# Four key places, a plan in fewer steps, and another order of layer 0's stores and layer 3's keys

## The reference

```python
x = x + tanh(g_xattn[0]) * L0_xattn(layernorm(x), ctx, ctx, mask)   # no projections, a mask
x = x + tanh(g_ffn[0]) * L0_ffn(layernorm(x), ...)
x = x + tanh(g_xattn[1]) * L1_xattn(layernorm(x), ctx, Wq, bq, Wk, bk, Wv, bv, Wo, bo)
x = x + tanh(g_ffn[1]) * L1_ffn(layernorm(x), Wr, W1, b1, W2, b2)   # top 2 of 8 experts
x = x + tanh(g_xattn[2]) * L2_xattn(layernorm(x), ctx, ...)
x = x + tanh(g_ffn[2]) * L2_ffn(layernorm(x), ...)                  # top 2 of 8 experts
x = x + tanh(g_xattn[3]) * L3_xattn(layernorm(x), ctx, ...)
x = x + tanh(g_ffn[3]) * L3_ffn(layernorm(x), ...)

# attention, every layer:
attn = softmax(einsum('bhqd,bhkd->bhqk', q, k) * scale)
out = einsum('bhqk,bhkd->bqhd', attn, v).reshape(B, S, 256) @ Wo + bo
# experts, layers 1 and 2:
w, ind = top_k(logits, 2)
out = sum over e of combine[:, e] * (gelu(x @ W1[e] + b1[e]) @ W2[e] + b2[e])
```

## Time and profile before

| | us |
|---|---|
| median of 3 runs | 1548.8 |
| fastest and slowest of them | 1547.69, 1549.62 |
| the profiled execution | 1545.74 |
| its span | 1543.9 |

### The profile page before, as it was taken

How to read it: one execution, slowest core, us unless ns; L and a number is a source line. 1 busy time by engine, 2 the same in 40 slices (tenths; PEclk the granted TensorE clock), 3 DMA queues, 4 the chain that set the end, 5 groups by cost and what they waited for, 6 DMA issues and landing times.

```text
span 1543.9 us, 29425 instructions
## 1 busy us (share of the span) xinstructions
PE 1312.7 (85%) x9497; PEld 955.5 (62%) x9524; DVE 960.3 (62%) x2651; ACT 860.8 (56%) x1718; POOL 721.0 (47%) x859
## 2 busy tenths in 40 slices
PE   2789889998998499999999899839999388995985
PEld 1445479855665289999986556628877245664333
DVE  6779753336985643333337688575544278967787
ACT  2456864434886245455535588535555156875564
POOL 4467440005642577777640564258994426532000
PEclk9999999997999699999999799969999798997998
DMA  9978030049761333343247975125444499710001
GB/s 274 285 153 166 12 100 1 1 130 220 137 140 52 103 123 124 117 149 126 76 148 241 222 129 109 35 89 155 147 132 166 146 259 201 141 28 1 0 14 41
DMA packets 116208, 188.86 MB, mean 122 GB/s; under 512 B 21552, under 2 KB 91824, under 8 KB 110256
## 3 DMA queue, kind: packets, MB, share of 16 engines
q0 software_dynamic: 37696, 105.19, 28.9%
q1 hardware_dynamic: 78368, 81.79, 16.8%
HBM read 128.17 MB, written 50.20 MB: 116 GB/s over the span
## 4 chain that ended last, share of the span: by engine, by line
PE 62%; DVE 14%; DMA 7%; POOL 6%; ACT 5%; issue 5%; SPq 1%; ACTq 0%; DVEq 0%; POOLq 0%
PE PS L1094 8%; PE PS L1253 8%; PE PS L1273 8%; PE PS L1047 8%; PE PS L1051 3%; PE PS L1131 2%; PE PS L1265 2%; DMA qk_parts<-q_parts 2%; PE PS L1074 2%; PE PS L1067 2%; PE PS L1107 2%; POOL weights L818 1%; PE PS L1154 1%; DMA y_tokens<-xng,into 1%; PE PS L911 1%
## 5 line engine op out<-in xcount | busy, mean ns | idle before, releaser
L2152 DVE TENSOR_REDUCE nm<-PS 128x2 f32<-128x512 f32 x384 | 250.3, 676 | 42.2 <-PE PS L1047 40.8
L1047 PE MATMUL PS<-stack 48*128 48x256 f32 x1024 | 212.3, 331 | 38.7 <-issue 10.8
L1047 PEld LDWEIGHTS PS<-stack 48*128 48x128 f32 x1024 | 151.6, 204 | 121.0 <-issue 61.6
L1051 PE MATMUL PS<-stack 49*128 49x256 f32 x1024 | 203.9, 322 | 1.0 <-ACT probs L1576 0.6
L1273 PE MATMUL PS<-weights,hh 128*128 x936 | 189.5, 292 | 3.8 <-DVE hl L2481 3.7
L1253 PE MATMUL PS<-weights,xh 128*128 x468 | 169.9, 418 | 11.3 <-DVE xl L2467 5.4
L1576 ACT ACTIVATE probs<-PS 128x512 f32<-128x512 f32 x256 | 145.0, 595 | 36.4 <-PE PS L1074 15.1
L709 POOL DMA_DIRECT2D stack<-mt x128 | 73.1, 571 | 185.4 <-ACT mt L1585 183.8
L1576 ACT ACTIVATE xng<-PS 128x512 f32<-128x512 f32 x256 | 145.3, 595 | 21.8 <-PE PS L1074 12.5
L1273 PEld LDWEIGHTS PS<-weights,hh 128*128 128x128 f32 x936 | 152.7, 193 | 5.4 <-issue 4.9
L1051 PEld LDWEIGHTS PS<-stack 49*128 49x128 f32 x1024 | 143.5, 195 | 10.5 <-ACT probs L1576 4.3
(11 more groups left out here) (335 smaller groups left out, 3079.9 us busy)
## 6 DMA issues: line engine op xcount, KB each, us to landing
stack<-qk_parts POOLq DMA_DIRECT2D x120, 256.0 KB, 4.1
stack<-qk_parts POOLq DMA_DIRECT2D x136, 128.0 KB, 3.7
qk_parts<-stack SPq DMA_DIRECT2D x32, 512.0 KB, 6.6
qk_parts<-q_parts SPq DMA_DIRECT2D x26, 512.0 KB, 5.3
weights<-W_dram POOLq DMA_DIRECT2D x12, 1024.0 KB, 7.0
wide<-ctxT_dram SPq DMA_DIRECT2D x16, 512.0 KB, 8.0
wslot<-y_tokens SPq DMA_DIRECT2D x16, 512.0 KB, 7.4
weights<-W_dram POOLq DMA_DIRECT2D x12, 512.0 KB, 5.1
```

What stands on the lines that cost most here:

```text
L1047: mm = pe.matmul(PS[:, u % 3, to], nat_q[:, at], nat_k, start=True, stop=True)
L1051: mm = pe.matmul(PS[:, 3 + v % 3, to], key_k[:, at], key_q, start=(l > 0 or half == 0), stop=(l > 0), skip_group_check=(l == 0))
L2152: nc.vector.tensor_reduce(nm[:, j % 2, at:at + 2], PS[:, (2 * t + h) % 3, :].rearrange("p (q n) -> p q n", q=2), AX.X, ALU.max, negate=Tru ...
```

## The change

It has four parts.

1. **Four key places, all layers.** `k_part(g)` lays the parts of groups 0 and 1 in the last slot of `stack` and those of 2 and 3 in the slot before. ACT and DVE no longer wait for the store of group g - 2; SP's `store_k` waits for it itself, for the sake of its semaphore. POOL waits for all key stores before it loads batch 2 (before: batch 3).
2. **Layer 0.** q1 stands in `probs` as in the other layers, and its store waits until batch 0 is loaded (stack_first); q2's and q3's halves wait for the rows of quads 0 to 3 (row_in). SP's order is k0 q0 k1 v0 k2 k3 q1, mask 2, q2, mask 3, v1, q3, v2 v3. PE's first scores ask for qlo_done 2, and DVE does the low part of q3 behind the first two maxima. ACT's first exp waits for q1's stores, which until now was so in layers 1 to 3 only.
3. **Planning.** The two choices go through one instruction where they took two; the chain of eight on `tile_e` becomes one comparison on 39 x 8 elements and one sum; `in_row` is made in two halves of 16, and PE multiplies the first while DVE makes the second; `into` moves behind the tables. POOL's gathers ahead wait: the third for the first to land, the fourth for the second, the fifth for the third and fourth, the seventh for the fifth and sixth.
4. **Layer 3.** All four groups' keys and values stand before the adds on PE, ACT and DVE. Layer 2 keeps the order of before.

```diff
+        def k_part(g, r):
+
+            two = stack[:, SLOTS - 1 - g // 2].rearrange("p q c n -> p (q c n)")
+            return two[:, g % 2 * 2048:(g % 2 + 1) * 2048].rearrange("p (r c n) -> p r c n", r=2, c=KC)[:, r]
...
-            if l and g == 1:
+            if g == 1:
                 return probs[:].rearrange("p a n -> p (a n)").rearrange("p (r c n) -> p r c n", r=2, c=KC)[:, r].bitcast(F32R)
...
                 sp.wait_ge(klo_done, GROUPS * l + g + 1)
+                if l or g >= 2:
+                    sp.wait_ge(*stored(k_out, l, g - 2))
...
-                if l and g >= 2:
+                if g >= 2:
                     sp.wait_ge(*stored(q_out, l, g - 2))
                 for r, part in enumerate((q_hi(l, g), q_lo(l, g))):
-                    if l and g == 1 and r == 0:
+                    if g == 1 and r == 0:
                         sp.wait_ge(stack_first, 144 * (l + 1))
-                    if l and g >= 2:
+                    if g >= 2:
                         j = QUADS * l + 2 * (g - 2) + r
                         sp.wait_ge(row_in[j % 4], 16 * (j // 4 + 1))
...
-                if at == 0 and b == SLOTS - 1:
+                if at == 0 and b == SLOTS - 2:
                     for g in range(GROUPS):
                         pool.wait_ge(*stored(k_out, l, g))
...
                     for i in range(AHEAD):
+                        if 2 <= i < 4:
+                            pool.wait_ge(xq_in[i - 2], 16 * l)
+                        elif i >= 4 and i % 2 == 0:
+                            pool.wait_ge(xq_in[i // 2], 32 * l)
                         gather(i, tile_in(i, i % 2)).then_inc(xq_in[i if i < 2 else 1 + i // 2], 16)
...
-                            pe.wait_ge(qlo_done, GROUPS)
+                            pe.wait_ge(qlo_done, 2)
                         pe.wait_ge(klo_done, GROUPS * (l + 1))
...
-                if l and n == 0:
+                if n == 0:
                     pe.wait_ge(qlo_done, GROUPS * (l + 1))
...
-                pe.wait_ge(hot_done, 2 * l - 1)
                 for j in range(2 * TILES):
+                    if j % TILES == 0:
+                        pe.wait_ge(hot_done, 3 * l - 2 + j // TILES)
...
-                if l and v == 0:
+                if v == 0:
                     act.wait_ge(*stored(q_out, l, 1))
...
-                for m in range(2):
-                    then(tt(eq[:, m], eq[:, m], where, ALU.mult))
-                    then(nc.vector.tensor_reduce(posf[:, m, :], eq[:, m], AX.X, ALU.add))
+                then(tt(eq[:], eq[:], where.unsqueeze(1).broadcast_to([P, 2, TILES, 8]), ALU.mult))
+                then(nc.vector.tensor_reduce(posf[:].rearrange("p m t -> p (m t)"), choices, AX.X, ALU.add))
...
-                for e in range(8):
-                    if e == 0:
-                        then(ts(tile_e[:, 0, :], iotas[:, 0:NT], escan[:, es, 0:1], None, ALU.is_ge))
-                    else:
-                        then(nc.vector.scalar_tensor_tensor(tile_e[:, e % 2, :], iotas[:, 0:NT], escan[:, es, e:e + 1],
-                                                            tile_e[:, 1 - e % 2, :], ALU.is_ge, ALU.add))
+                begun = late[:].rearrange("p i d -> p (i d)")[:, 0:8 * NT].rearrange("p (n e) -> p n e", e=8)
+                then(tt(begun, iotas[:, 0:NT].unsqueeze(2).broadcast_to([P, NT, 8]),
+                        upto.unsqueeze(1).broadcast_to([P, NT, 8]), ALU.is_ge))
+                then(nc.vector.tensor_reduce(tile_e[:, 1, :], begun, AX.X, ALU.add))
...
-                keys_low(l + 1, 0)
+                for g in range(GROUPS if l == 2 else 1):
+                    keys_low(l + 1, g)
```

More of the change, by code:

```diff
@@ L411, in q_place @@
         def q_place(l, g):
-            return stored(q_out, l, g - 4 if l and g == 3 else g - 2)
+            return stored(q_out, l, g - 4 if g == 3 else g - 2)
         def rows_of(n, r, g):
@@ L508, in load_v @@
                                      io["ctx"][g * 512:(g + 1) * 512, :].rearrange("(t p) d -> p t d", p=P)).then_inc(x_in[g], 16)
-                    for g in range(GROUPS):
-                        if g == 2:
-                            load_v(0)
-                            sp.wait_ge(mask_done, 1)
-                            load_mask(2)
-                        store_k(0, g)
-                        store_q(0, g)
+                    store_k(0, 0)
+                    store_q(0, 0)
+                    store_k(0, 1)
+                    load_v(0)
+                    store_k(0, 2)
+                    store_k(0, 3)
+                    store_q(0, 1)
+                    sp.wait_ge(mask_done, 1)
+                    load_mask(2)
+                    store_q(0, 2)
                     sp.wait_ge(mask_done, 2)
                     load_mask(3)
-                    for g in range(1, GROUPS):
+                    load_v(1)
+                    store_q(0, 3)
+                    for g in range(2, GROUPS):
                         load_v(g)
@@ L1507, in features @@
                 act.wait_ge(xT_mm, GROUPS * 2 * l + g + 1)
-                if l == 0 and g >= 2:
+                if l == 0 and g == 2:
                     act.wait_ge(*q_place(l, g))
@@ L1545, in project @@
                     u = 2 * l
-                    keys(l, 0)
-                    values(l, 0)
+                    for g in range(GROUPS if l == 3 else 1):
+                        keys(l, g)
+                        values(l, g)
                     for g in range(GROUPS - 1):
-                        keys(l, g + 1)
+                        if l == 2:
+                            keys(l, g + 1)
                         group_roots(u, g)
-                        values(l, g + 1)
+                        if l == 2:
+                            values(l, g + 1)
                         if g == 1:
@@ L2327, in route, with rows_from @@
                 assert k == ROUTE
-            def rows_of_tiles(l, k, first, part, block):
+            def rows_from(l, k, first, part, block):
                 n = part.shape[1]
@@ L2339, in rows_of_tiles, with rows_to @@
                 nc.vector.scalar_tensor_tensor(idx[:, at], block, float(P), tmp(1), ALU.mult, ALU.add).then_inc(idx_done, 1)
+                return k + 2
+            def rows_to(l, k, first, part, block):
+                n = part.shape[1]
+                at = slice(first, first + n)
+                tmp = lambda r: scan[:, 0].rearrange("p t e -> p (t e)")[:, 32 * (r + 1):32 * (r + 1) + n]
                 nc.vector.scalar_tensor_tensor(tmp(2), block, 0.5, pad_row[:, at], ALU.is_lt, ALU.mult).then_inc(route_v[l], 1)
-                dve.wait_ge(route_v[l], k + 3)
-                tt(tmp(0), part, tmp(2), ALU.add).then_inc(route_v[l], 1)
-                dve.wait_ge(route_v[l], k + 4)
+                dve.wait_ge(route_v[l], k + 1)
+                nc.vector.tensor_tensor(tmp(0), part, tmp(2), ALU.add).then_inc(route_v[l], 1)
+                dve.wait_ge(route_v[l], k + 2)
                 nc.vector.scalar_tensor_tensor(into[:, at], block, float(P), tmp(0), ALU.mult, ALU.add).then_inc(placed, 1)
-                return k + 4
+                return k + 2
             def plan(l):
@@ L2451, in plan_late @@
                 dve.wait_ge(idx_mm, 2 * l)
-                rows_of_tiles(l, k, AHEAD, PS[:, 7, 0:rest], PS[:, 7, rest:2 * rest])
+                k = rows_from(l, k, AHEAD, PS[:, 7, 0:rest], PS[:, 7, rest:2 * rest])
+                rows_to(l, k, AHEAD, PS[:, 7, 0:rest], PS[:, 7, rest:2 * rest])
             def sparse(l):
@@ L2521, in sparse @@
                     group_variances(2 * l + 2, g)
-                    if g + 1 < GROUPS:
+                    if g + 1 == GROUPS:
+                        queries(l + 1, 0)
+                    elif l == 1:
                         keys_low(l + 1, g + 1)
-                    else:
-                        queries(l + 1, 0)
                     group_scales(2 * l + 2, g)
```

61 lines of the change are left out of this document (28 added, 33 removed).

## The result

| | before | after |
|---|---|---|
| median, 18 runs each | 1547.76 us | 1537.35 us |
| profiled execution | 1545.74 | 1539.33 |
| ratio, 95% interval | | 0.9931 (0.9916 to 0.9946) |

The kernel is 10.4 us faster by the medians. Two later jobs, on chips 7 and 9, gave 0.9889 (0.9865 to 0.9913) and 0.9935 (0.9908 to 0.9962) for the same two kernels. The forecast was 1537, with a gain of 12.2.

The account below looks back on a forecast made before the run. PE (62% of the span) bounds it, so edits pay only where PE waits at the end of a DVE, DMA or ACT chain. 4 + 1.2 + 0.3 + 1.4 + 5.3 = 12.2 gives 1537 us, range 1530 to 1544.5.

Parts of the forecast that it names:

- Layer 0, 4 forecast: Layer 0: new store order lets q3 land before mask 3, shortening PE's stall; gain 4 us, bounds -2 to 7.5.
- The first steps: Layer 0: scores near 37, q1 landing 15.4 us later at 56.5, first exp at 57.8, 2.6 us late.
- the old stall: Layer 0: PE stood 4.96 us until 81.72 behind POOL's mask 3 wait; stall and slow clock cost 7.3 us.
- the second rival: Layer 0 gives nothing: first exp 7 to 9 us late, freed stall spent; total 1540.6, chance 0.2.
- Planning of layer 1, 1.2 forecast: Layer 1: tables 2.1 us earlier, PE then waits for its first gather; gain 1.2 us, range 0.5 to 2.1.
- Planning of layer 2, 0.3 forecast: Layer 2: waits between POOL's gathers delay the weights, shrinking the front's 1.2 us to 0.3, range -1 to 1.4.
- the front: Layer 2 planning: same earlier start as layer 1, first gather 0.45 us sooner, worth 1.2 us before gather waits.
- Start of layer 2, 1.4 forecast: Layer 2: four places remove DVE's 1.39 us wait for ACT's key part; gain 1.4 us, range 0 to 1.4.
- Start of layer 3, 5.3 forecast: Layer 3: keys and values move into PE's 24.69 us idle hole, shortening DVE's rounds; gain 5.3 us, range 3.7 to 6.
- A round: Layer 3: one group's DVE round of adds without keys_low, 6.66 us where it took 7.61.
- The loss to the low clock: Layer 3: PE slow after a longer pause, one product 1.6 us too long, mostly under DVE's rounds; 5.7 becomes 5.3.
- a sign of being wrong: Layer 3: PE's queries running at the low clock on DVE's heels would show the forecast wrong.

Follow-up runs that it names:

- y2_hold: Changed kernel with SP held in layer 0 after q3's stores until quad 6's maxima landed, mask 4 ahead of v2, v3: 1540.98 us, ratio 0.9927.
- x1_places: Kernel before with the four key places alone, including SP's own waits and POOL's earlier key-store wait: 1544.33 against 1549.42 us, ratio 0.9973.
- z1_old_layer0: Changed kernel with layer 0's part undone; four places, planning and layer 3's order kept: 1540.87 against 1547.18 us, ratio 0.9963.
- y1_free: Changed kernel without the waits between POOL's gathers ahead: 1535.48 us, ratio 0.9906.
- z2: Changed kernel with layer 0's part undone and without the waits between the gathers ahead: 1537.76 us, ratio 0.994.

## Why the prediction was right, and which term was not

**The total** was right: 12.2 forecast, 10.4 measured, and 10.2 as the sum of the stretches in the table (1.4 + 1.8 + 1.5 + 0.1 + 5.4). That it comes so near is in part luck. Layer 0's own part gave nothing of its 4, and a gain there that the sum had at nothing, 2.2 from the places, stood in for some of it; and two of the five differences, layer 0's and layer 1's, are of the size by which single traces of one kernel differ, so their sum is known to 1 or 2 us at best. The pair of profiles alone, 6.4 apart, would have looked like half of it: the profiled execution of after lies 2.0 above its median and that of before 2.0 below, and one product at the low clock in layer 1 is 1.6 of it.

**Layer 0, 4 forecast: 1.4 measured, and not for the reason given.** The first steps held: scores near 37 (38.15), q1's landing by what is queued ahead of it, 56.5 (57.2), first exp 57.8 (58.5), mask 3 no longer waited for, and the step behind it short. PE passed the old stall 4.2 us earlier in this pair of traces (82.00 against 86.18); over the traces above it is 2.9. What I left out is what the sum priced at 0: everything behind. I followed each transfer to its own landing and asked who waits for that; I didn't ask what the transfers that now come together (q3, v2, v3, masks 4 and 5) do to a 4 KB store of row maxima issued among them. It took 8.9 us, and PE waited; with the transfers held back (y2_hold) it took 1.9. So the part gives what it saved back within three quads. The 1.4 that layer 0 shows come with the four places, which I had put at nothing there: x1_places and z1_old_layer0 have 2.2 in the mean without the new order. That POOL's earlier wait for all key stores is the way of it is likely but not shown. "Layer 0 gives nothing", the second rival, is what happened to that part, by another way than its late exps.

**Planning of layer 1, 1.2 forecast: 1.8** by the mean to tile 10, inside 0.5 to 2.1, with ranges that overlap (92.8 to 95.0 without, 90.3 to 94.4 with). Where the traces repeat, it is less: 0.4 at PE's tile 0, where I had 0.9, and 0.9 to 1.0 at ACT's first high part. The tables came 1.9 sooner, as worked out (2.1), but the first gather, which PE now waits for, only 0.1, where I had 0.45.

**Planning of layer 2, 0.3 forecast: 0.1.** The mechanism was right, the waits between the gathers take the front's gain, but both sides of it were larger than in my sum. The front is not "the same" as in layer 1: the first gather comes 2.0 sooner in the mean, where I had 0.45, and PE's tile 0 2.7, where I had 1.2; why so much more than in layer 1 no run took apart. And y1_free and z2 show the price of the waits, 2.2 us. From the first gather to the end of the last I had put 13.4 us; it took 14.3.

**Start of layer 2, 1.4 forecast: 1.5.**

**Start of layer 3, 5.3 forecast: 5.4** to the first exp, 5.7 to the fourth adds. A round was forecast at 6.66 and is 6.67. The loss to the low clock was put at 0.4 and is 0.3 in the mean of ten traces. In the trace of after it is much more: there the first exp stands 53.0 behind the first adds, a gain of 3.9, and in the nine others 50.6 to 52.1. PE after the pause, in the timeline of after:

```profile
1233.47 1.97 PE L926 MATMUL PS<-ident,xng 128*128 128x128 f32 x8 [15.31 <-ACT xng L1518]
1237.80 5.41 PE L966 MATMUL PS<-wide,wproj 128*128 128x512 f32 x8 [2.36 <-ACT wide L1529]
...
1248.91 10.10 PE L966 MATMUL PS<-wide,wproj 128*128 128x512 f32 x16 [1.01 <-ACT wide L1529]
```

transposes at 1.97 instead of 1.04, products at 5.41 and 10.10 instead of 3.6 and 7.1. The first lies under DVE's rounds. The second, queries at a granted clock of 0.70 right behind DVE, is what the prediction had named as a sign of being wrong; it is there in this trace, and most of the 1.8 that this trace lacks of 5.7 would be it (my reading).

## What to carry to other kernels

Where the DMA engines are full, price a reordering of transfers not only by when each lands but by the smallest one issued among them: a 4 KB store that an engine waits for took 1.7 to 10 us in layer 0 here, by what was under way. Work moved out of a round of a chain (layer 3's keys) is worth its own rows, and such a term can be forecast to a few tenths (5.3 against 5.4, 6.66 against 6.67). A wait put in for one resource (the gathers' landings) is paid by whatever stands behind it in the same queue: here it ate 2.2 us of a front gain of 2.7. And before a stretch full of matmuls is compared, it has to be seen in several traces of one kernel.

## What the runs showed of the hardware

Executions of one kernel on one chip spread over some 16 us here (1541 to 1557 in 29 runs of the kernel before on chip 9), and a part of that is PE's granted clock: the same product behind the same wait of 2.25 us took 3.60 us at a granted clock of 1.00, or 5.23 at 0.69. I had taken the traces to repeat within tenths, as the stretches of DVE in layer 3 do (20.0 in ten traces); stretches full of matmuls don't (layer 1's exps, first to last, 96 to 102 us). No such stretch could be compared by one pair of traces.
